# A curvature-flow stage on Trainium2: the step is clipped and the image rounded on GpSimd, the update comes one slot later, and the mixed derivative last

## Chip, cores and metric

One core of a Trainium2 chip. The metric is the device time of one execution in microseconds (us); lower is better. Everything is float32; the stencil matmuls read rounded copies in the format fp32r.

## Reference

Four blocks follow one another on a batch of 16 images of 16 channels and 32 x 32 pixels: an attention block with large weights (some 160 MB are read), two residual convolution blocks, and the curvature flow that the change is mostly about:

```python
def step(u, _):
    ux, uy, uxx, uxy, uyy = _derivs(u)          # Sobel stencils, each clipped to +-10
    g2 = ux * ux + uy * uy
    denK = jnp.maximum(1.0 + g2, EPS)
    K = jnp.clip((uxx * uyy - uxy * uxy) / (denK * denK + EPS), -5.0, 5.0)
    denH = jnp.sqrt(1.0 + g2 + EPS)
    H = ((1.0 + uy*uy) * uxx - 2.0 * ux*uy*uxy + (1.0 + ux*ux) * uyy) / (2.0 * denH**3 + EPS)
    H = jnp.clip(H, -5.0, 5.0)
    diff = jnp.clip(alpha * K + beta * H, -1.0, 1.0)
    u = u + DT * diff
    u = jnp.pad(u[:, :, 1:-1, 1:-1], ((0, 0), (0, 0), (1, 1), (1, 1)), mode='edge')
    return (u, None)
u, _ = jax.lax.scan(step, x, None, length=10)
return 0.7 * u + 0.3 * x
```

## The kernel before

**Weights and convolutions.** SyncE streams the weights through a ring of four 4 MB slots. TensorE consumes them (`thin`, L373); the last 16 blocks `s_` are the output projection. Between them the four convolution layers run in four waves of image columns (`conv`, matmuls at L497 and L502, relu L954 on ScalarE, add L776 on VectorE). `halo_rows` copies border rows between partition groups (L81, L85, L942), and `convs_after(s_)` says which layer follows which block. The last wave can only begin when the last block has arrived.

**Into the curvature stage.** `chunk_rows` (L509) gathers the images into four chunks `x` of 128 partitions (4 channels x 32 rows) by 32 columns x 16 images, the first half of the columns ahead of the last wave and the second behind it; L948, L864 and L1023 copy them out of PSUM into `u`. An image is held as a rounded high part (`u_hi`) and the rest (`u_lo`, L1076, GpSimd), so that two fp32r matmuls give nearly full precision. The stencil matrices are loaded by SyncE and cast to fp32r on GpSimd (L1070).

**The slots.** 10 steps x 4 chunks are 40 slots `k`. A slot of TensorE (`fields`, L548) is 34 matmuls of 480 columns: UXY 8, UX 4 and UY 6 (signal `fld1`), then UYY and UXX 16 (`fld2`), in that order. Each of the other engines runs its own `slot_step(k)` in which the front of slot k ("new") and the end of slot k-1 ("old") are interleaved in a written order; semaphores of the same names tie the engines together. The names are used in what follows:
- VectorE: `num0` L804 (old), `clip1` L807, `clipxy` L809, `clip2` L813, `kh` L820 (old), `slope` L825, `outer` L829, `cross` L835, then `diff` L841, `clipd` L844 and the update `u` L850 (old). clip1, clip2, kh and outer have 960 columns, the others 480.
- ScalarE: `p2` L986, `sqr` L987, `pad` L968 and the rounding `hi` L979 of the chunk for slot k+2, `up_h` L995, `end_k` L996, `ends` L1000 (old), `sqxy` L1005, `lnw` L1007, `psq` L1008, `w15` L1010, `lnd` L1013, `inv` L1016, and in the first four slots `x3` L1019 (0.3 u for the result).
- GpSimd: `absum` L1086 and `hn` L1088 (old, behind the update u of the slot before), `cxy` L1091, `m` L1093, `lo` L1076.

`num0` waits for `sqxy` and `m` of the slot before, `kh` for `hn` and `inv`, `diff` for `ends`, TensorE's next-but-one slot for `kh`. Two sets of buffers and of PSUM banks alternate (`q`, `n`).

**The tail.** TensorE applies the edge rule (L590), VectorE adds 0.3 x (L878, "finish"), SyncE stores.

## Time and profile before

| | us |
|---|---|
| median of 3 runs | 792.9 |
| lowest, highest | 789.88, 798.36 |
| the profiled execution, its own time | 793.43 |
| its span, first to last instruction | 791.6 |
| busy: TensorE, VectorE, ScalarE, GpSimd | 661.2, 463.0, 391.0, 269.1 |

The span is what the profile shows; the time has 1.8 us around it. The busy times are over the whole span, in which the first half is bound by weight transfers (DMA 32% of the chain that ended last); the curvature stage fills roughly the second half. In the views below a time is counted from the span's start.

### The profile page before, as it was taken

Reading aid. Unit: us, or ns where it says so; the run is one execution under the profiler, and the core shown is the slowest. Engines: PE = TensorE matmul, PEld = TensorE weight load, DVE = VectorE, ACT = ScalarE, POOL = GpSimd, SP = SyncE. Lnnn points to the kernel's source line nnn. Section 1 sums busy time; section 2 is a strip of 40 time slices with the busy share of each in tenths; the row PEclk is TensorE's granted clock in tenths of the full one; section 3 lists DMA queues with packets and bytes.
Section 4 is the critical chain, followed back from the end, with each engine's and each line's share of the span. In section 5 each row is a group of like instructions: output and inputs, shape, how many; then the busy total and the mean of one; then the engine's idle time right before and its main releaser. Section 6 shows DMA issues by size and latency. Waiting matters only on the chain.

```text
span 791.6 us, 11654 instructions
## 1 busy us (share of the span) xinstructions
PE 661.2 (84%) x4644; PEld 488.1 (62%) x4644; DVE 463.0 (58%) x668; ACT 391.0 (49%) x654; POOL 269.1 (34%) x231
## 2 busy tenths in 40 slices
PE   5896999998955588878789988989989988998983
PEld 3773874663522255555577777777767777777770
DVE  5630000491301022223253899999999999999996
ACT  1300000330000010111122899999999999999994
POOL 1000000000026000000011666776776677677662
PEclk9999999999986899999999999999999999999996
...
DMA packets 20804, 166.57 MB, mean 210 GB/s; under 512 B 1824, under 2 KB 1952, under 8 KB 11424
## 3 DMA queue, kind: packets, MB, share of 16 engines
...
## 4 chain that ended last, share of the span: by engine, by line
DMA 32%; PE 30%; ACT 16%; DVE 16%; issue 5%; POOL 1%; DVEq 0%; POOLq 0%; ACTq 0%; SPq 0%
DMA ring<-wout_w 19%; PE bank L548 10%; PE bank L359 6%; PE bank L419 4%; PE bank L474 3%; DMA ring<-wv_w 3%; PE bank L373 3%; DMA ring<-wv_p 3%; DMA ring<-wout_p 3%; DMA ring<-wqk_p 3%; DVE ring L820 3%; ACT ring L1000 3%; DVE ring L807 2%; ACT ring L996 2%; ACT bank L987 2%
## 5 line engine op out<-in xcount | busy, mean ns | idle before, releaser
L548 PE MATMUL bank<-u_parts,vmr 128*128 128x480 f32 x1360 | 305.3, 382 | 38.6 <-DVE ring L820 37.6
L548 PEld LDWEIGHTS bank<-u_parts,vmr 128*128 128x128 f32 x1360 | 252.7, 188 | 91.3 <-DVE ring L820 52.9
L373 PE MATMUL bank<-ring,small 128*32 128x256 f32 x1152 | 79.7, 426 | 36.0 <-DMA ring<-wout_w 32.1
L1086 POOL TENSOR_TENSOR ring<-ring 128x480 f32<-128x480 f32 x40 | 49.1, 1228 | 99.5 <-DVE reg_a L850 77.1
L373 PEld LDWEIGHTS bank<-ring,small 128*32 128x32 f32 x1152 | 37.9, 120 | 72.0 <-DMA ring<-wout_w 32.0
L373 PE MATMUL bank<-ring,xw 128*32 128x256 f32 x1024 | 62.3, 402 | 17.1 <-DMA ring<-wv_w 17.1
L784 DVE STREAM_TRANSPOSE reg_b<-bank 128x256 f32<-128x256 f32 x16 | 7.2, 450 | 109.7 <-PE bank L373 109.7
L942 ACT ACTIVATE reg_e<-xa 32x384 f32<-32x384 f32 (+9 forms) x16 | 8.3, 522 | 112.7 <-DVE xa L787 83.8
L671 DVE SCALAR_TENSOR_TENSOR reg_a<-bank,prm 128x512 f32<-128x512 f32 x4 | 2.8, 692 | 102.9 <-PE bank L426 102.9
L359 PE MATMUL bank<-reg_a,ring 128*128 128x256 f32 x256 | 57.9, 389 | 5.7 <-ACT reg_a L896 3.4
L373 PEld LDWEIGHTS bank<-ring,xw 128*32 128x32 f32 x1024 | 33.7, 115 | 43.8 <-DMA ring<-wv_w 20.8
L359 PEld LDWEIGHTS bank<-reg_a,ring 128*128 128x128 f32 x256 | 49.6, 195 | 13.3 <-issue 3.5
L1070 POOL CAST vmr<-ring 128x3328 fp32r<-128x3328 f32 x1 | 3.0, 2957 | 151.5 <-DMA ring<-edge 151.5
L1042 POOL MEMSET reg_d<- 128x2176 f32 x1 | 1.9, 1923 | 149.0 <-PE bank L426 149.0
L1088 POOL TENSOR_TENSOR ring<-ring 128x480 f32<-128x480 f32 x40 | 49.0, 1225 | 3.1
L1091 POOL TENSOR_TENSOR ring<-ring 128x480 f32<-128x480 f32 x40 | 48.8, 1219 | 3.4 <-DVE ring L807 3.4
L1093 POOL TENSOR_TENSOR ring<-ring 128x480 f32<-128x480 f32 x40 | 48.7, 1218 | 3.3 <-DVE ring L813 3.3
L807 DVE TENSOR_SCALAR ring<-bank 128x960 f32<-128x960 f32 x40 | 46.1, 1151 | 5.0 <-PE bank L548 5.0
L813 DVE TENSOR_SCALAR ring<-bank 128x960 f32<-128x960 f32 x40 | 46.0, 1149 | 2.7 <-PE bank L548 2.7
L820 DVE TENSOR_TENSOR ring<-ring,bank 128x960 f32<-128x960 f32 x40 | 45.8, 1146 | 0.9 <-POOL ring L1088 0.9
L829 DVE SCALAR_TENSOR_TENSOR ring<-bank,ring 128x960 f32<-128x960 f32 x40 | 46.0, 1149 | 0.0
L1076 POOL TENSOR_TENSOR u_parts<-reg_a,u_parts 128x512 fp32r<-128x512 f32 (+1 forms) x30 | 39.6, 1320 | 18.0 <-ACT u_parts L974 18.0
(186 smaller groups left out, 1020.7 us busy)
## 6 DMA issues: line engine op xcount, KB each, us to landing
...
```

Source lines behind the costliest of these rows:

```text
L359: ins = te.matmul(bank[:, 4 + n % 2, (h % 2) * TOK:(h % 2 + 1) * TOK], half[2 * (k % NSLOT) + h // 4][:, c, h % 4 * DH:(h % 4 + 1) * DH], ...
L373: ins = te.matmul(bank[32 * j:32 * j + 32, b_, n0:n0 + 256], lhs(c), slot[k % NSLOT][:, c, 256 * j:256 * j + 256], start=start and c == 0, ...
L548: last = te.matmul(dst[:, 0:NF], mat(m, first), p3[:, 2 + off:S + off, :], start=(high and n == 0), stop=(not high and n == len(terms) - 1))
L807: v.tensor_scalar(f(q, 0, 2).rearrange("p (x n) -> p x n", x=2), fields_in(q, 0, 2), 10.0, -10.0, ALU.min, ALU.max).then_inc(ve["clip1"], 1)
L813: v.tensor_scalar(f(q, 3, 2).rearrange("p (x n) -> p x n", x=2), bank[:, 3:5, 0:NF], 10.0, -10.0, ALU.min, ALU.max).then_inc(ve["clip2"], 1)
L820: v.tensor_tensor(kh[n].rearrange("p (x n) -> p x n", x=2), num[n].rearrange("p (x n) -> p x n", x=2), fields_in(n, 0, 2), ALU.mult).then_ ...
L829: v.scalar_tensor_tensor(ab[q].rearrange("p (x n) -> p x n", x=2), fields_in(q, 0, 2), 1.0, f(q, 3, 2).rearrange("p (x n) -> p x n", x=2), ...
L1076: p.tensor_tensor(u_lo[c][:, at], u[c][:, at], u_hi[c][:, at].bitcast(F32), ALU.subtract).then_inc(po["lo"], 1)
L1086: p.tensor_tensor(abs_[n], ab[n][:, 0:NF], ab[n][:, NF:2 * NF], ALU.add).then_inc(po["absum"], 1)
L1088: p.tensor_tensor(num[n][:, NF:2 * NF], abs_[n], cxy[n], ALU.add).then_inc(po["hn"], 1)
L1091: p.tensor_tensor(cxy[q], fld[q][:, 0:NF], fld[q][:, NF:2 * NF], ALU.mult).then_inc(po["cxy"], 1)
L1093: p.tensor_tensor(mxy[q], fld[q][:, 3 * NF:4 * NF], fld[q][:, 4 * NF:5 * NF], ALU.mult).then_inc(po["m"], 1)
```

## The change

It reorders the slot and moves two pieces of work to GpSimd.
- `clipd` becomes one GpSimd `tensor_scalar` (subtract `mid`, min DT); the other limit goes into the update, which is now max(dif, -DT) + u. `dif` gets two buffers.
- The update u of slot k-2 is made in slot k, between clip1 and clip2, instead of in slot k-1 at the end. GpSimd waits for it behind the clip.
- The rounding `hi` is a GpSimd copy ahead of `lo`, instead of a ScalarE step.
- `ends` is written to PSUM, into the bank of the mixed term (`mixed`), and `diff` reads it there. `diff` stands ahead of `cross`, which is now the slot's last step.
- TensorE makes UXY last in a slot (signal `fldxy`); clipxy is behind kh. On ScalarE, sqxy is behind w15.
- The stencil matrices go by a DMA of GpSimd's queue straight to `vmr`; the cast is gone.
- Convolution layer 1 follows layer 0 within one block, the first halves of the chunks are gathered one block earlier, the second halves chunk by chunk, and high and low parts are made by halves (FIRST, SECOND).
- The edge rule and the finish work on 30 columns and two rim columns; the last chunk goes in two parts.

The diff, cut to its core (8 leading blanks taken off):

```diff
@@ -64,7 +64,7 @@
     if s == NO - 1:
 return [(WAVES - 1, layer) for layer in range(NCONV)]
-    return [(w, s - G + 1 - G * w) for w in range(WAVES - 1) if 0 <= s - G + 1 - G * w < NCONV]
+    return [(w, layer) for w in range(WAVES - 1) for layer in range(NCONV) if s == G * (w + 1) - 1 + max(layer - 1, 0)]
 def halo_rows(eng, copy, shifts, w, layer, source, waits, halo_sem):
...
+def parts(x):
+    return [(2, S)] if x < NCH - 1 else [(2, S // 2 + 1), (S // 2 + 1, S)]
...
-vm = ring[:, la[0]:la[0] + NVM]
...
-end_k, up_h, end_h = dual(NF), dual(NF), dual(NF)
-dif = reg_b[:, 0:NF]
+end_k, up_h, dif = dual(NF), dual(NF), dual(NF)
 assert la[0] <= NSLOT * SLOTF
...
@@ -514,31 +526,33 @@
         i, m = s_ // NSLOT, s_ % NSLOT
         te.wait_ge(ve["bank_turn"], s_ + 1)
         thin(k1 + s_, lambda c: wft[:, c * 2 * B:(c + 1) * 2 * B], 4 + m, 0, True, True, s_ == NO - 1)
-        if s_ == NO - 1:
+        if s_ == NO - 2:
             te.wait_ge(po["pick"], 1)
             te.wait_ge(ve["conv"], pairs_done(WAVES - 2, NCONV - 1, 1))
             for x in range(NCH):
-                te.wait_ge(ve["bank_turn"], NO + x + 1)
+                te.wait_ge(ve["bank_turn"], NO + min(x, 2) + 1)
                 for g in range(G):
                     ins = chunk_rows(x, g, 0)
                 ins.then_inc(pe["chunk"], 1)
         for w, layer in convs_after(s_):
             if layer == 0:
                 te.wait_ge(ve["stage"], G * (w + 1))
+            if (w, layer) == (WAVES - 1, 0):
+                te.wait_ge(ac["u_in"], NCH)
...
     te.wait_ge(ac["u_in"], NCH)
-    for h in range(2):
-        te.wait_ge(ve["conv"], pairs_done(WAVES - 1, NCONV - 1, h))
-        for x in range(NCH):
-            for g in (2 * h, 2 * h + 1):
-                ins = chunk_rows(x, g, 1)
-            if h:
-                ins.then_inc(pe["chunk"], 1)
+    te.wait_ge(ve["bank_turn"], NO + NSLOT)
+    for x in range(NCH):
+        for g in range(G):
+            if x == 0 and g % 2 == 0:
+                te.wait_ge(ve["conv"], pairs_done(WAVES - 1, NCONV - 1, g // 2))
+            ins = chunk_rows(x, g, 1)
+        ins.then_inc(pe["chunk"], 1)
...
-        te.wait_ge(ac["hi"], k)
-        if reuse:
-            te.wait_ge(ve["num"], k - 2)
-        stencil(bank[:, b1 + 2, :], u_hi[c], first, UXY, True)
-        te.wait_ge(po["lo"], k)
-        stencil(bank[:, b1 + 2, :], u_lo[c], first, UXY, False)
+        if first:
+            te.wait_ge(ac["hi"], k)
+        else:
+            te.wait_ge(po["hi"], k - NCH)
         if reuse:
             te.wait_ge(ve["kh"], k - 2)
-        for n, terms in enumerate((UX, UY)):
-            stencil(bank[:, b1 + n, :], u_hi[c], first, terms, True)
-            ins = stencil(bank[:, b1 + n, :], u_lo[c], first, terms, False)
-        ins.then_inc(pe["fld1"], 1)
+        stencil(bank[:, b1, :], u_hi[c], first, UX, True)
+        te.wait_ge(po["lo"], k)
+        stencil(bank[:, b1, :], u_lo[c], first, UX, False)
+        stencil(bank[:, b1 + 1, :], u_hi[c], first, UY, True)
+        stencil(bank[:, b1 + 1, :], u_lo[c], first, UY, False).then_inc(pe["fld1"], 1)
...
-    te.wait_ge(po["vm"], 1)
-    te.wait_ge(ld_vm, 32)
+        if reuse:
+            te.wait_ge(ve["diff"], k - 2)
+        stencil(bank[:, b1 + 2, :], u_hi[c], first, UXY, True)
+        stencil(bank[:, b1 + 2, :], u_lo[c], first, UXY, False).then_inc(pe["fldxy"], 1)
+    te.wait_ge(ld_vm, 16)
...
-        te.wait_ge(ac["pad"], SLOTS - NCH + x + 1)
-        te.matmul(bank[:, EDGE_BANK[x], :], edge_m, u_in(x), start=True, stop=True).then_inc(pe["edge"], 1)
+        te.wait_ge(ve["u"], SLOTS - NCH + x + 1)
+        for n, (a_, b_) in enumerate(parts(x)):
+            te.matmul(bank[:, EDGE_BANK[x] + n, 0:(b_ - a_) * B], edge_m, u[x][:, a_ * B:b_ * B],
+                      start=True, stop=True).then_inc(pe["edge"], 1)
...
         n = 1 - q
+        mixed = lambda s_: fields_in(s_, 2)[:, 0, :]
         if old:
             v.wait_ge(po["m"], k - 1)
             v.wait_ge(ac["sqxy"], k - 1)
-            v.tensor_tensor(num[n][:, 0:NF], mxy[n], fields_in(n, 2)[:, 0, :], ALU.subtract).then_inc(ve["num"], 1)
+            v.tensor_tensor(num[n][:, 0:NF], mxy[n], mixed(n), ALU.subtract).then_inc(ve["num"], 1)
...
-            v.tensor_scalar(fields_in(q, 2)[:, 0, :], fields_in(q, 2)[:, 0, :], 10.0, -10.0,
-                            ALU.min, ALU.max).then_inc(ve["clipxy"], 1)
+        if before:
+            v.wait_ge(po["clipd"], k - 2)
+            if first and k - 2 <= NCH:
+                v.wait_ge(ac["x3"], k - 2)
+            inner = u[c][:, 2 * B:S * B]
+            v.scalar_tensor_tensor(inner, dif[q], -DT, inner, ALU.max, ALU.add).then_inc(ve["u"], 1)
...
+            v.wait_ge(pe["fldxy"], k)
+            v.tensor_scalar(mixed(q), mixed(q), 10.0, -10.0, ALU.min, ALU.max).then_inc(ve["clipxy"], 1)
...
+        if old:
+            v.wait_ge(ac["ends"], k - 1)
+            v.scalar_tensor_tensor(dif[n], end_k[n], ten_ab[:, 0:1], mixed(n),
+                                   ALU.min, ALU.add).then_inc(ve["diff"], 1)
+        if new:
             v.wait_ge(po["cxy"], k)
             v.wait_ge(ve["clipxy"], k)
-            v.scalar_tensor_tensor(cxy[q], cxy[q], -2.0, fields_in(q, 2)[:, 0, :],
-                                   ALU.mult, ALU.mult).then_inc(ve["cross"], 1)
-        if not old:
-            return
-        v.wait_ge(ac["ends"], k - 1)
-        v.scalar_tensor_tensor(dif, end_k[n], ten_ab[:, 0:1], end_h[n],
-                               ALU.min, ALU.add).then_inc(ve["diff"], 1)
-        v.wait_ge(ve["diff"], k - 1)
-        v.tensor_scalar(dif, dif, high_lim, low_lim, ALU.min, ALU.max).then_inc(ve["clipd"], 1)
-        v.wait_ge(ve["clipd"], k - 1)
-        if first and k - 1 <= NCH:
-            v.wait_ge(ac["x3"], k - 1)
-        inner = u[c][:, 2 * B:S * B]
-        v.scalar_tensor_tensor(inner, dif, mid, inner, ALU.subtract, ALU.add).then_inc(ve["u"], 1)
+            v.scalar_tensor_tensor(cxy[q], cxy[q], -2.0, mixed(q), ALU.mult, ALU.mult).then_inc(ve["cross"], 1)
...
+    def finish(x):
+        v.wait_ge(ac["x3"], x + 1)
+        x3c = x3[:, x, :].rearrange("p (w b) -> p w b", b=B)
+        for n, (a_, b_) in enumerate(parts(x)):
+            v.wait_ge(pe["edge"], x + n + 1)
+            got = bank[:, EDGE_BANK[x] + n, 0:(b_ - a_) * B].rearrange("p (w b) -> p w b", b=B)
+            inner = x3c[:, a_ - 1:b_ - 1, :]
+            v.scalar_tensor_tensor(inner, got, 0.7, inner, ALU.mult, ALU.add).then_inc(ve["fin"], 1)
...
+                  halo_waits(w, layer), ac["halo"])
+        if (w, layer) == (WAVES - 1, NCONV - 1):
+            a.wait_ge(pe["slot_used"], U_ALL)
+            a.wait_ge(ac["u_in"], NCH)
+            for x in range(NCH):
+                a.activation(u_hi[x][:, FIRST], u[x][:, FIRST], ACT.Copy).then_inc(ac["hi_first"], 1)
...
-            a.activation(u_hi[c], u[c], ACT.Copy).then_inc(ac["hi"], 1)
+            a.activation(u_hi[c][:, SECOND], u[c][:, SECOND], ACT.Copy).then_inc(ac["hi"], 1)
...
         pad(k - NCH, c)
-        a.wait_ge(ac["pad"], k - NCH)
-        a.wait_ge(pe["fld2"], k - NCH)
-        a.activation(u_hi[c][:, B:(S + 1) * B], u_in(c), ACT.Copy).then_inc(ac["hi"], 1)
...
-            a.activation(end_h[n], up_h[n], ACT.Relu, bias=ten_ab[:, 1:2],
+            a.activation(fields_in(n, 2)[:, 0, :], up_h[n], ACT.Relu, bias=ten_ab[:, 1:2],
                          scale=neg_b).then_inc(ac["ends"], 1)
...
-        a.wait_ge(ve["cross"], k)
-        a.activation(fields_in(q, 2)[:, 0, :], fields_in(q, 2)[:, 0, :], ACT.Square).then_inc(ac["sqxy"], 1)
         a.wait_ge(ve["slope"], k)
         a.activation(lnw[q], slope[q], ACT.Ln, bias=D_EPS).then_inc(ac["lnw"], 1)
         a.activation(den[q][:, 0:NF], slope[q], ACT.Square).then_inc(ac["psq"], 1)
         a.wait_ge(ac["lnw"], k)
         a.activation(den[q][:, NF:2 * NF], lnw[q], ACT.Exp, bias=LN2, scale=1.5).then_inc(ac["w15"], 1)
+        a.wait_ge(ve["cross"], k)
+        a.activation(fields_in(q, 2)[:, 0, :], fields_in(q, 2)[:, 0, :], ACT.Square).then_inc(ac["sqxy"], 1)
...
-    p.wait_ge(ld_vm, 32)
-    p.tensor_copy(vmr[:, :], vm).then_inc(po["vm"], 1)
+    p.wait_ge(pe["slot_used"], U_ALL)
+    p.dma_start(vmr[:, :], vmats).then_inc(ld_vm, 16)
+    p.wait_ge(ac["hi_first"], NCH)
+    p.wait_ge(ac["halo"], 2 * WAVES * NCONV)
+    p.wait_ge(ve["halo"], 4 * WAVES * NCONV)
+    for x in range(NCH):
+        p.tensor_tensor(u_lo[x][:, FIRST], u[x][:, FIRST], u_hi[x][:, FIRST].bitcast(F32),
+                        ALU.subtract).then_inc(po["lo_first"], 1)
...
-        p.wait_ge(ac["hi"], k)
-        at = slice(B, (S + 1) * B) if later else slice(0, ROWF)
+        at = slice(B, (S + 1) * B) if later else SECOND
+        if later:
+            p.wait_ge(ac["pad"], k - NCH)
+            p.wait_ge(pe["fldxy"], k - NCH)
+            p.tensor_copy(u_hi[c][:, at], u[c][:, at]).then_inc(po["hi"], 1)
+            p.wait_ge(po["hi"], k - NCH)
+        else:
+            p.wait_ge(ac["hi"], k)
         p.tensor_tensor(u_lo[c][:, at], u[c][:, at], u_hi[c][:, at].bitcast(F32),
                         ALU.subtract).then_inc(po["lo"], 1)
...
         if old:
-            if after:
-                p.wait_ge(ve["u"], k - 2)
-            p.wait_ge(ve["cross"], k - 1)
+            p.wait_ge(ve["outer"], k - 1)
             p.tensor_tensor(abs_[n], ab[n][:, 0:NF], ab[n][:, NF:2 * NF], ALU.add).then_inc(po["absum"], 1)
             p.wait_ge(po["absum"], k - 1)
+            p.wait_ge(ve["cross"], k - 1)
             p.tensor_tensor(num[n][:, NF:2 * NF], abs_[n], cxy[n], ALU.add).then_inc(po["hn"], 1)
+        if before:
+            p.wait_ge(ve["diff"], k - 2)
+            if k == 3:
+                p.wait_ge(ve["scales"], 1)
+            p.tensor_scalar(dif[q], dif[q], mid, DT, ALU.subtract, ALU.min).then_inc(po["clipd"], 1)
+            p.wait_ge(ve["u"], k - 2)
```

## Rows read from the trace of the kernel before

**Rows 1.** Windows view, a stretch of the curvature stage; engine, busy us, instructions.

```profile
600.00:650.00 50.00, 44.25 (x198) 36.51 (x197) 49.31 (x65) 48.10 (x77) 34.91 (x29) 1.00 0.00 0
```

**Rows 2.** Timeline, vector engine: start, length, engine, line, operation, tiles.

```profile
600.52 1.15 DVE L820 TENSOR_TENSOR ring<-ring,bank 128x960 f32<-128x960 f32 x1
...
609.12 1.15 DVE L820 TENSOR_TENSOR ring<-ring,bank 128x960 f32<-128x960 f32 x1
```

**Rows 3.** Timeline of one early slot, all engines; brackets give idle time and releaser.

```profile
444.44 1.14 DVE L820 TENSOR_TENSOR ring<-ring,bank 128x960 f32<-128x960 f32 x1
...
445.96 0.59 ACT L995 ACTIVATE ring<-ring 128x480 f32<-128x480 f32 x1
...
446.46 0.77 ACT L996 ACTIVATE ring<-ring,small 128x480 f32<-128x480 f32 x1
...
447.32 0.79 ACT L1000 ACTIVATE ring<-ring,small 128x480 f32<-128x480 f32 x1
448.02 0.55 ACT L1005 ACTIVATE bank<-bank 128x480 f32<-128x480 f32 x1
...
448.51 0.58 ACT L1007 ACTIVATE ring<-ring 128x480 f32<-128x480 f32 x1
...
449.46 0.72 DVE L850 SCALAR_TENSOR_TENSOR reg_a<-reg_b,small,reg_a 128x480 f32<-128x480 f32 x1
449.49 0.59 ACT L1010 ACTIVATE ring<-ring 128x480 f32<-128x480 f32 x1
450.10 0.65 DVE L804 TENSOR_TENSOR ring<-ring,bank 128x480 f32<-128x480 f32 x1
...
450.26 1.23 POOL L1086 TENSOR_TENSOR ring<-ring 128x480 f32<-128x480 f32 x1 [2.77 <-DVE reg_a L850]
450.67 1.15 DVE L807 TENSOR_SCALAR ring<-bank 128x960 f32<-128x960 f32 x1
...
451.58 1.23 POOL L1088 TENSOR_TENSOR ring<-ring 128x480 f32<-128x480 f32 x1
451.73 0.66 DVE L809 TENSOR_SCALAR bank<-bank 128x480 f32<-128x480 f32 x1
...
453.36 1.15 DVE L820 TENSOR_TENSOR ring<-ring,bank 128x960 f32<-128x960 f32 x1
...
455.11 1.30 POOL L1076 TENSOR_TENSOR u_parts<-reg_a,u_parts 128x512 fp32r<-128x512 f32 x1
```

**Rows 4.** Timeline of the first slot: the mixed term's square and its reader.

```profile
439.35 0.56 ACT L1005 ACTIVATE bank<-bank 128x480 f32<-128x480 f32 x1 [3.46 <-DVE ring L835]
...
440.01 0.66 DVE L804 TENSOR_TENSOR ring<-ring,bank 128x480 f32<-128x480 f32 x1 [0.69 <-ACT bank L1005]
```

**Rows 5.** GpSimd's groups by line: busy us, mean ns, idle before.

```profile
L1070 POOL CAST vmr<-ring 128x3328 fp32r<-128x3328 f32 x1 | 3.0, 2957 | 151.5 <-DMA ring<-edge 151.5
...
L1064 POOL COPY prm<-prm 128x128 f32<-128x128 f32 x1 | 0.3, 302 | 0.0
```

**Rows 6.** Timeline from the last weights to the first stencils.

```profile
399.37 1.91 PE L509 MATMUL bank<-xa,prm 128*32 128x256 f32 x32
...
407.00 3.62 DVE L85 COPY reg_f<-reg_d 16x480 f32<-16x480 f32 x2
...
410.77 1.63 PE L502 MATMUL bank<-reg_f,xw 96*128 96x160 f32 x8 [1.74 <-DVE reg_f L85]
...
414.12 1.06 DVE L85 COPY reg_e<-xa 16x528 f32<-16x528 f32 x2
...
429.17 15.87 PE L548 MATMUL bank<-u_parts,vmr 128*128 128x480 f32 x72 [0.22 <-POOL u_parts L1076]
```

**Rows 7.** Timeline of the tail.

```profile
780.58 1.16 DVE L820 TENSOR_TENSOR ring<-ring,bank 128x960 f32<-128x960 f32 x1 [0.89 <-POOL ring L1088]
781.77 0.60 ACT L995 ACTIVATE ring<-ring 128x480 f32<-128x480 f32 x1 [1.52 <-DVE ring L820]
...
788.49 0.69 DVE L878 SCALAR_TENSOR_TENSOR ring<-bank,ring 128x512 f32<-128x512 f32 x1 [1.89 <-PE bank L590]
```

More of the change, by code:

```diff
@@ L85, in halo_rows, with chunk_bank @@
         copy(halo[dw * QUAD:dw * QUAD + C, 0:G - 1, at], cols(slice(0, C), 1, G, dw)).then_inc(halo_sem, 1)
+def parts(x):
+    return [(2, S)] if x < NCH - 1 else [(2, S // 2 + 1), (S // 2 + 1, S)]
+def chunk_bank(x, half):
+    return 4 + x if half or x < NCH - 1 else 0
 def pairs_done(w, layer, h):
@@ L186, in build @@
         dt_ab, five_ab, ten_ab = (sm(2) for _ in range(3))
-        neg_b, mid, low_lim, high_lim = (sm(1) for _ in range(4))
+        neg_b, mid = (sm(1) for _ in range(2))
         wft = sm(KC * 2 * B)
@@ L201, in build @@
             "pl_sq_sums", "pln", "negmax", "prob", "pf", "dsl", "stage", "conv", "bank_turn", "img",
-            "clip1", "clipxy", "clip2", "num", "slope", "outer", "cross", "kh", "diff", "clipd", "u", "scales", "fin", "halo", "u_in")}
+            "clip1", "clipxy", "clip2", "num", "slope", "outer", "cross", "kh", "diff", "u", "scales", "fin", "halo", "u_in")}
         ac = {n: sem("ac_" + n) for n in (
             "order", "patch_sq", "patch_std", "fl", "win_sq", "win_std", "pl_std", "qkv", "vt", "exp", "pt", "rows",
-            "wwk", "wv", "conv", "p2", "sqr", "sqxy", "lnw", "psq", "w15", "lnd", "inv", "end_k", "up_h", "ends", "x3", "pad", "hi", "halo", "u_in")}
-        po = {n: sem("po_" + n) for n in ("zero", "bandz", "pick", "vm", "padz", "lo", "cxy", "m", "absum", "hn")}
+            "wwk", "wv", "conv", "p2", "sqr", "sqxy", "lnw", "psq", "w15", "lnd", "inv", "end_k", "up_h", "ends", "x3", "pad", "hi", "hi_first", "halo", "u_in")}
+        po = {n: sem("po_" + n) for n in ("hi", "clipd", "zero", "bandz", "pick", "padz", "lo", "lo_first", "cxy", "m", "absum", "hn")}
         ld_last, st_out = [sem(f"ld_last{n}") for n in range(NPIECE)], sem("st_out")
@@ L582, in _ @@
                     fields(i * NCH + (c + 1), c, False, True)
+            te.wait_ge(ld_edge, 16)
             for x in range(NCH):
@@ L857, in _ @@
             then(v.tensor_scalar(neg_b, dt_ab[:, 1:2], -1.0, None, ALU.mult))
-            then(v.tensor_tensor(mid, five_ab[:, 0:1], five_ab[:, 1:2], ALU.add))
-            then(v.tensor_scalar(low_lim, mid, DT, None, ALU.subtract))
-            v.tensor_scalar(high_lim, mid, DT, None, ALU.add).then_inc(ve["scales"], 1)
+            v.tensor_tensor(mid, five_ab[:, 0:1], five_ab[:, 1:2], ALU.add).then_inc(ve["scales"], 1)
             for x in range(1, NCH, 2):
@@ L1098, in _ @@
                 low(x + 1, x, False)
-            for k in range(1, LOOP_FROM):
-                slot_step(k, k % 2, (k + 1) % NCH, True, k > 1, k > 2, k + 2 > NCH)
-            with p.Fori(1, LOOPS + 1) as i:
-                for m in range(NCH):
-                    slot_step(i * NCH + (m + 3), (m + 3) % 2, (m + 4) % NCH, True, True, True)
-            for k in range(LOOP_END, SLOTS + 2):
-                slot_step(k, k % 2, None, k <= SLOTS, True, True)
+            for k in range(1, SLOTS + 3):
+                slot_step(k, k % 2, (k + 1) % NCH if k + 2 <= SLOTS else None, k <= SLOTS, 1 < k <= SLOTS + 1, k > 2, k + 2 > NCH)
     return nc
```

53 lines of the change are left out of this document (28 added, 25 removed).

## Prediction, made before the changed kernel was run

> **What bounds the kernel now.** I read the busy times of a stretch in the middle of the curvature stage first: of 50 us the vector engine is busy 49.3, ScalarE 48.1, TensorE 44.3 and GpSimd 34.9 [rows 1]. Two engines are nearly full, so the view of busy times can't say what a lighter load on one of them is worth; that depends on who waits for whom. Next the timeline: the same instruction of the vector engine, the product `kh` (L820), starts every 8.60 us [rows 2]. The stage is 40 such slots, and what counts is the period. The last view is one slot read start to start, since instructions of one engine overlap by a tenth of a microsecond and their printed lengths add up to too much [rows 3]. Start to start, a vector step of 960 columns takes 1.06 (450.67 to 451.73), one of 480 takes 0.57 (450.10 to 450.67), and `u`, with two operands in SBUF, 0.64 (449.46 to 450.10) [rows 3]. Before the stage, the chip waits for the output weights and then for the last wave of convolutions; behind it there is one serial tail.
>
> **The vector engine's own work.** The change takes `clipd` (L844) from it and the second SBUF operand from `diff`. What is left is clip1, clip2, kh and outer at 1.06, num0, clipxy, slope, diff and cross at 0.57, and u at 0.64: 4.24 + 2.85 + 0.64 = 7.73 us, 0.87 under the period of now. If nothing else became late, 38 slots of that would be worth 33 us. ScalarE loses the rounding `hi` (L979, some 0.6 with its launch), so it has room too.
>
> **The wait that takes the place.** `num0` of slot k+1 needs the square of the mixed term, `sqxy(k)`, from ScalarE, which needs `cross(k)`. Before, cross was followed on the vector engine by diff, clipd and u, which hid the square. After, cross is the last step of slot k and num0 the first of the next, with nothing between. And on ScalarE, sqxy is no longer ahead of lnw but behind `up_h`, `end_k`, `ends`, `lnw`, `psq` and `w15`, all in order. The first of these waits for kh. That closes a ring, and I count round it, from the start of kh(k-1), start to start where an engine follows itself:
> kh to the start of up_h: 1.15 long [rows 3] and 0.03 to get across, as in the last slot, where ScalarE waited for it (780.58 + 1.16 to 781.77 [rows 7]), so 1.18; up_h to end_k 0.50, end_k to ends 0.86 (it drains first), ends to the next instruction 0.70 [rows 3]. With PSUM as target I take 0.65: `sqxy` in PSUM takes 0.55 to 0.56 against 0.58 to 0.60 for the like work into SBUF [rows 3, 4]. lnw and psq together 0.98 (448.51 to 449.49), w15 0.49, the half of that [rows 3]. sqxy to the start of num0: 0.66 [rows 4], the only place before where the vector engine waited for it. Then num0 0.57, clip1 1.06, u 0.64, clip2 1.06 [rows 3], and kh(k) may start.
> Sum: 1.18 + 0.50 + 0.86 + 0.65 + 0.98 + 0.49 + 0.66 + 0.57 + 1.06 + 0.64 + 1.06 = 8.65. The only term without a row is ends into PSUM, 0.60 to 0.70, which makes 8.60 to 8.70. So the vector engine gets 7.7 us of work in a slot and stands idle 0.9 us, ahead of num0. I expect 8.65 where 8.60 was.
>
> **GpSimd.** It takes two instructions more. The rounding copy of 512 columns has a price from two rows: a copy of 128 columns takes 0.302 and the cast of 3,328 takes 2.957 [rows 5], 0.83 ns a column, so 0.62. The clip (`tensor_scalar`, 480 columns, one scalar from memory) has no row. Its lower end is the same line, 0.59. Its upper end is the two-operand step, 1.23 [rows 3], with 0.09 for the scalar from memory (end_k, with two such scalars, takes 0.77 where up_h takes 0.59 [rows 3]), so 1.32. It streams one tensor, as the copies do, and so I take 0.59 + 0.09 = 0.68.
> The Trainium skill (GPSIMD Engine Reference, Engine selection) speaks against moving elementwise work here: two-input work is about twice as slow as on VectorE, while one-input work goes at roughly line rate. By its first half the clip would be the 1.23 of the rows, by its second half near the copies' line; the trace has the two-operand steps at 1.23 and no clip, so it bears out the first and leaves the second open for this operation. The first would make the time 799.6, the second leaves it at 788.6.
> Two rings go through GpSimd. One: u start to cxy 0.80 (449.46 to 450.26, since GpSimd waits for u), cxy and m 1.18 each (451.58 to 455.11 is three steps at 1.18), hi 0.62 + 0.08, lo 1.27 (its 1.30 less the overlap), absum 1.32, hn 1.18, then the clip X and 0.08 to u: 7.71 + X [rows 3]. Two: outer 1.15 + 0.08, absum 1.32, hn 1.18, X + 0.08, u 0.64, clip2 1.06, kh 1.06, clipxy and slope 1.14: 7.71 + X again. With X = 0.68 both give 8.39, hidden under 8.65; they decide from X = 0.94 on, and their cover is 0.26 us. Behind the clip in GpSimd's queue are cxy, m, hi and lo, and for these wait cross, num0 and TensorE two slots on; the fields of slot k+2 have more than 5 us of slack, since u one slot later still comes 2 slots ahead of its use.
>
> **TensorE.** It issues the same 34 matmuls a slot in another order. 72 of them ran without a break in 15.87 us [rows 6], 0.22 each, so 7.5 us a slot, below every ring. UXY last means it waits for diff(k-2) and clip2(k-1), but is needed only by clipxy, a step after kh. I price that at nothing; the cover is about 3.9 us of lead.
>
> **Start of the stage.** Three gains. (a) The first half of the images is gathered one weight block earlier, while DMA is the bound. Of the 32 passes with 1.91 us at 399.37 [rows 6] about 0.8 stood past the point where the convolution could begin (estimate; ends 0.4 to 1.9). (b) The cast of the stencil matrices, 2.96 us on GpSimd, goes away. It became possible when the matrices had landed, just then two small halo copies of the vector engine (407.00) took 3.62 us, and a like pair later 1.06; TensorE was idle for 1.74 on them [rows 5, 6]. That the two engines were in each other's way is my reading. Gain 1.7, or nothing if it was something else. The matrices come by a DMA from GpSimd's queue to their final place instead; the 22 us from 407.00 to 429.17 hide it. (c) Chunks in order of x, and a second-half-only rounding: the first low part is ready about 1.1 sooner, and 64 matmuls between it and the second clip2 become 58 (estimate from the order: 6 x 0.22 = 1.3). Together 0.8 + 1.7 + 2.4 = 4.9, so kh(1), at 444.44 [rows 3], comes at 439.5.
>
> **The slots.** kh(39) is 38 periods on: 439.5 + 38 x 8.65 = 768.2. The four slots in which ScalarE also stores 0.3 u ran at 8.92 before (444.44 to 453.36 [rows 3]) and don't now, since ScalarE has about 7.7 of own work. That is 1.0 us of the gain. kh(40) comes without clip1 and clip2 in the way: about 7.3 on, 775.5, against 780.58 [rows 7].
>
> **The tail.** Before, from kh(40) to the end of the last vector step 788.49 + 0.69 - 780.58 = 8.60 [rows 7]. After: ends' result at 3.3, diff to 4.0, finish(0) and finish(1) in the vector queue to 5.5 (the clip on GpSimd ends at 4.8 and is hidden), u to 6.2, two edge matmuls of 240 columns at about 1.0 each, then finish: 8.9. So 0.3 is lost; smaller last transfers may give it back. Last vector step at 784.4, plus the 2.4 of the output DMA before (span 791.6 less 789.18): span 786.8. The profiled execution took 793.43 for 791.6 of span, so 1.8 more: 788.6. That stands against 793.43 of the profiled execution and against the median of 792.9.
>
> **The rivals.**
> Forecast (chance 0.60): the ring over sqxy, 8.60 to 8.70 a slot, 788.6; with the start's bounds 785 to 792.
> GpSimd becomes the bound (0.14). Mechanism: the clip costs as a two-operand step and u waits for it. Point of decision X = 0.94. With 1.23 the period is 8.94 and the time 788.6 + 38 x 0.29 = 799.6; with 1.32 it is 9.03 and 803. This is slower than before. For it speaks that no GpSimd arithmetic at less than 1.22 is on record in this trace, against it the copies.
> The mixed square isn't late (0.14). If sqxy ran beside the rest, or ScalarE's steps were closer together than in the slow first slots, GpSimd at 8.39 would be next: 788.6 - 38 x 0.26 = 778.7. Half of that, 784, is as possible. Against it speaks the code: the order on both engines is fixed.
> The start gives nothing (0.12). Mechanism: GpSimd's descriptor work for the matrices and its four early low parts run beside the same vector copies as the cast did, so gains (b) and part of (c) don't come: 791 to 794.
> The Trainium skill (SBUF — State Buffer, Who interferes with whom) has GpSimd and a two-port VectorE operation exclude each other; by its rule the descriptors, not the vector copies, could be the ones to wait, and the time would stay at the forecast.
>
> **How the numbers follow.** About 1% (8 us) is what a measurement of this kernel can tell from no change. The faster side (under 785) takes most of the third rival and a little of the forecast: 0.22. The slower side (over 801) takes the upper half of the second and a little for what I missed: 0.13. The range 779 to 802 holds the forecast, the fourth, and all but the ends of the others.
>
> **What would show it.** In the profile after: the vector engine idle about 0.9 us ahead of num0 in each slot, released by ScalarE's square; vector engine busy near 90%, ScalarE near 90%, GpSimd above 85%; kh every 8.65; the chain of waits alternating between ScalarE's six steps and num0, clip1, u, clip2, kh. kh(1) near 439.5, halo copies at 1.1 a pair. I am wrong if u waits for GpSimd's clip (X over 0.94), if hi takes over 0.9, or if kh comes sooner than every 8.6.

## The result, and the profile after

| | before | after |
|---|---|---|
| median, us | 794.07 (4 runs, 789.88 to 798.36) | 833.08 (4 runs, 830.67 to 835.23) |
| the profiled execution, us | 793.43 | 833.83 |
| its span, us | 791.6 | 832.0 |

The kernel after takes 1.050 times as long as the one before [1.046, 1.0535, the 95% interval]. The forecast was 788.6, the range 779 to 802.

The page of the kernel after: busy times, and three groups of the list by line (busy us and mean ns of one, then the engine's idle time ahead of them and what ended it).

```profile
PE 690.2 (83%) x4646; PEld 511.7 (61%) x4646; DVE 441.6 (53%) x632; ACT 362.0 (44%) x618; POOL 364.8 (44%) x311
...
L562 PE MATMUL bank<-u_parts,vmr 128*128 128x480 f32 x1360 | 323.3, 398 | 58.0 <-DVE ring L848 57.3
...
L1133 POOL TENSOR_SCALAR ring<-ring,small 128x480 f32<-128x480 f32 x40 | 75.5, 1888 | 4.8 <-DVE ring L865 4.8
...
L1125 POOL TENSOR_TENSOR ring<-ring 128x480 f32<-128x480 f32 x40 | 49.0, 1226 | 7.9 <-DVE ring L859 6.1
```

L1133 is the clip on GpSimd: 1.89 us, the only GpSimd step above 1.3 in the slot, and more than the two-input sum of the same 480 columns (L1125, 1.23). One slot of the timeline, the steps around it (start us, length us, engine, line; in brackets the idle time before and its releaser); it answers to [rows 2, 3]:

```profile
619.24 1.14 DVE L848 TENSOR_TENSOR ring<-ring,bank 128x960 f32<-128x960 f32 x1
...
620.44 7.62 PE L562 MATMUL bank<-u_parts,vmr 128*128 128x480 f32 x34 [0.58 <-DVE ring L848]
620.55 0.61 POOL L1113 CAST u_parts<-reg_a 128x512 fp32r<-128x512 f32 x1
...
621.80 0.76 ACT L1030 ACTIVATE bank<-ring,small 128x480 f32<-128x480 f32 x1
622.49 0.59 ACT L1035 ACTIVATE ring<-ring 128x480 f32<-128x480 f32 x1
...
624.01 1.24 POOL L1128 TENSOR_TENSOR ring<-ring 128x480 f32<-128x480 f32 x1
...
624.62 0.65 DVE L827 TENSOR_TENSOR ring<-ring,bank 128x480 f32<-128x480 f32 x1 [0.76 <-ACT bank L1040]
...
625.22 1.89 POOL L1133 TENSOR_SCALAR ring<-ring,small 128x480 f32<-128x480 f32 x1
...
627.14 0.66 DVE L838 SCALAR_TENSOR_TENSOR reg_a<-ring,reg_a 128x480 f32<-128x480 f32 x1 [0.80 <-POOL ring L1133]
...
627.89 1.20 POOL L1138 TENSOR_TENSOR ring<-ring 128x480 f32<-128x480 f32 x1 [0.78 <-DVE reg_a L838]
...
628.79 1.15 DVE L848 TENSOR_TENSOR ring<-ring,bank 128x960 f32<-128x960 f32 x1
```

From `kh` (L848) to `kh` are 9.55 us where 8.60 were. Inside the slot both waits are to be seen: `num0` (L827) waits 0.76 for the square, forecast as about 0.9, and `u` (L838) waits 0.80 for the clip, which the forecast had hidden and the prediction had named as the sign that it is wrong; GpSimd then waits 0.78 for `u`. That the second sets the period is what experiments 1 and 2 show. From 600 to 650 us VectorE is busy 42.0 us, ScalarE 38.2 and GpSimd 44.6: 84%, 76% and 89%, where near 90%, near 90% and above 85% were forecast. The view of waits, whole span (total us, times, longest):

```profile
PE bank L562 <- DVE ring L848: 57.3, 38, 2.3
...
DVE ring L827 <- ACT bank L1040: 30.3, 40, 0.8
...
DVE reg_a L838 <- POOL ring L1133: 25.0, 30, 1.8
```

The other 10 of the 40 updates go to `reg_g` and wait 7.9 us more.

**The balance.** kh(1) comes at 445.28 (before 444.44 [rows 3]), kh(39) at 812.02, kh(40) at 820.46 (before 780.58 [rows 7]); the span ends 11.54 later (before 11.02). So 0.84 + 39.04 + 0.52 = 40.4 us, all that lies between 793.43 and 833.83, nearly all of it in the slots. Of the 38 intervals from kh(1) to kh(39), 25 take 9.53 to 9.55 and 13 take 9.83 to 9.88. The view by stretches shows what is with 12 of the 13 (the other, the 15th, has a clock of 1.00 and comes up in experiment 6); here a usual interval and the long one after it (busy us of each engine, PEclk, DMA share, GB/s):

```profile
464.40:473.90 9.50, 7.63 (x34) 6.30 (x34) 7.94 (x11) 7.98 (x13) 8.50 (x8) 1.00 0.00 0
473.90:483.80 9.90, 8.60 (x32) 7.35 (x33) 8.09 (x12) 7.45 (x12) 8.85 (x8) 0.83 0.00 0
```

In the 12 the granted clock is 0.83 in the mean (for part of the interval 1.2 GHz, the lower level), after TensorE had waited 2.0 us for kh (L848) at 475.20; the fields come late and clip2 (L841) waits for them at its end:

```profile
475.20 8.99 PE L562 MATMUL bank<-u_parts,vmr 128*128 128x480 f32 x33 [2.01 <-DVE ring L848]
...
482.71 1.16 DVE L841 TENSOR_SCALAR ring<-bank 128x960 f32<-128x960 f32 x1 [0.25 <-PE bank L562]
```

**The start.** The halo copies that took 3.62 [rows 6] take 1.00, and the matmuls behind them no longer wait: the cast had been in their way. But the first convolution of the last wave takes 5.50 us where the same 24 matmuls took 3.21, at a clock of 0.50 (1.2 GHz):

```profile
402.78 1.94 PE L385 MATMUL bank<-ring,small 128*32 128x256 f32 x16 [0.53 <-DMA ring<-wout_w]
...
405.61 5.50 PE L509 MATMUL bank<-xa,reg_c 128*128 128x144 f32 x24 [0.90 <-DVE xa L809]
...
413.70 1.00 DVE L85 COPY reg_f<-reg_d 16x480 f32<-16x480 f32 x2
```

```profile
400.00:410.00 10.00, 8.26 (x50) 5.58 (x51) 2.55 (x6) 1.12 (x2) 0.57 (x1) 0.50 0.46 164
```

### The profile page after: what moved, and what is told of

It reads as the page before. It is cut to its first block, busy times and chain, and to the rows that moved or that the text cites. A ratio compares the mean times of both kernels' runs of the same rounds, so it can differ in the third digit from the quotient of the medians.

```text
span 832.0 us, 11664 instructions
## 1 busy us (share of the span) xinstructions
PE 690.2 (83%) x4646; PEld 511.7 (61%) x4646; DVE 441.6 (53%) x632; ACT 362.0 (44%) x618; POOL 364.8 (44%) x311
## 4 chain that ended last, share of the span: by engine, by line
PE 36%; DMA 27%; POOL 20%; DVE 12%; issue 4%; ACT 1%; SPq 0%; POOLq 0%; DVEq 0%; ACTq 0%
DMA ring<-wout_w 18%; PE bank L562 12%; PE bank L371 7%; POOL ring L1133 6%; PE bank L385 5%; POOL ring L1128 4%; POOL ring L1125 4%; DVE ring L848 4%; PE bank L486 4%; PE bank L431 3%; DMA ring<-wv_w 3%; DMA ring<-wout_p 3%; DMA ring<-wqk_p 3%; PE bank L509 2%; DVE ring L841 2%
## 5 line engine op out<-in xcount | busy, mean ns | idle before, releaser
L562 PE MATMUL bank<-u_parts,vmr 128*128 128x480 f32 x1360 | 323.3, 398 | 58.0 <-DVE ring L848 57.3
L562 PEld LDWEIGHTS bank<-u_parts,vmr 128*128 128x128 f32 x1360 | 267.0, 199 | 114.4 <-issue 59.2
L1133 POOL TENSOR_SCALAR ring<-ring,small 128x480 f32<-128x480 f32 x40 | 75.5, 1888 | 4.8 <-DVE ring L865 4.8
L371 PE MATMUL bank<-reg_a,ring 128*128 128x256 f32 x256 | 61.9, 407 | 5.9 <-ACT reg_a L925 3.4
L371 PEld LDWEIGHTS bank<-reg_a,ring 128*128 128x128 f32 x256 | 52.4, 206 | 14.9 <-issue 3.5
L1025 ACT ACTIVATE ring<-ring 128x480 f32<-128x480 f32 x40 | 24.2, 605 | 77.5 <-DVE ring L848 77.5
L1125 POOL TENSOR_TENSOR ring<-ring 128x480 f32<-128x480 f32 x40 | 49.0, 1226 | 7.9 <-DVE ring L859 6.1
L841 DVE TENSOR_SCALAR ring<-bank 128x960 f32<-128x960 f32 x40 | 46.1, 1153 | 5.5 <-PE bank L562 5.5
```

What stands on the lines that cost most here:

```text
L371: ins = te.matmul(bank[:, 4 + n % 2, (h % 2) * TOK:(h % 2 + 1) * TOK], half[2 * (k % NSLOT) + h // 4][:, c, h % 4 * DH:(h % 4 + 1) * DH], ...
L562: last = te.matmul(dst[:, 0:NF], mat(m, first), p3[:, 2 + off:S + off, :], start=(high and n == 0), stop=(not high and n == len(terms) - 1))
L841: v.tensor_scalar(f(q, 3, 2).rearrange("p (x n) -> p x n", x=2), bank[:, 3:5, 0:NF], 10.0, -10.0, ALU.min, ALU.max).then_inc(ve["clip2"], 1)
L1125: p.tensor_tensor(abs_[n], ab[n][:, 0:NF], ab[n][:, NF:2 * NF], ALU.add).then_inc(po["absum"], 1)
L1133: p.tensor_scalar(dif[q], dif[q], mid, DT, ALU.subtract, ALU.min).then_inc(po["clipd"], 1)
```

## The experiments

Each was run beside the kernel before (its median 794.75, 795.34 and 793.32 us in the three groups). In later kernels the line numbers are a few higher or lower.

**1. The clip back on VectorE (v_clip).** All else is as changed.

```diff
-  # GpSimd, slot k:
-    p.wait_ge(ve["diff"], k - 2)
-    p.tensor_scalar(dif[q], dif[q], mid, DT, ALU.subtract, ALU.min).then_inc(po["clipd"], 1)
+  # VectorE, last in slot k, behind cross:
+    v.wait_ge(ve["diff"], k - 1)
+    v.tensor_scalar(dif[n], dif[n], mid, DT, ALU.subtract, ALU.min).then_inc(ve["clipd"], 1)
```

> The changed kernel with one thing undone: the clip (subtract, min) is a VectorE instruction again, last in the slot behind cross, and leaves GpSimd. Theory A (GpSimd's clip of 1.89 us is the whole loss; behind it stands the ring over the square sqxy): the clip falls into the 0.76 us that VectorE waits ahead of num0, the period goes from 9.54 to 8.65, GpSimd's own ring is about 7.7; the time is 445.3 (first kh) + 38 x 8.65 + 7.3 + 10.4 (tail) + 1.8 = 793. Theory B (the later update and the rounding copy load GpSimd too much, whatever the clip): the period stays above 9.2 and the time above 815. Theory C (VectorE and GpSimd are in each other's way once an SBUF-to-SBUF clip of VectorE runs beside absum and hn): the clip stretches by up to 1.2 us, the period is 9.1 to 9.4, the time 810 to 822.

792.76 us, ratio 0.997 [0.995, 1.000]. Every interval is 8.65 to 8.67: the ring over the square, counted as 8.65. The clip takes 0.47 on VectorE and lies in the wait for the square, of which 0.38 is left:

```profile
614.30 0.47 DVE L874 TENSOR_SCALAR ring<-ring,small 128x480 f32<-128x480 f32 x1
...
615.15 0.66 DVE L827 TENSOR_TENSOR ring<-ring,bank 128x480 f32<-128x480 f32 x1 [0.38 <-ACT bank L1043]
```

So the clip on GpSimd makes all of the loss; the rest of the change is worth about nothing. Theory A had 793; of theory C there is no sign, since every clip of this run took 0.46 or 0.47.

**2. The square early (sq_early).** The clip stays on GpSimd; cross goes ahead of diff, and the square ahead of lnw.

```diff
   # VectorE
+  cross; then diff              (was: diff; then cross)
   # ScalarE
+  a.activation(mixed, mixed, ACT.Square).then_inc(ac["sqxy"], 1)
   a.activation(lnw[q], slope[q], ACT.Ln, bias=D_EPS).then_inc(ac["lnw"], 1)
   ...
-  a.activation(mixed, mixed, ACT.Square).then_inc(ac["sqxy"], 1)   # was behind w15
```

> The changed kernel with the order of the mixed term's square undone and the clip left on GpSimd: cross ahead of diff on VectorE, sqxy ahead of lnw on ScalarE. Theory A (GpSimd's ring decides, sqxy's wait of 0.76 us lies under it): the wait ahead of num0 goes away, the wait ahead of u grows by as much (from 0.80 to 1.5), the period stays at 9.54 and the time at 831 to 834. Rival (the wait for sqxy is what costs): the period falls by 0.6 to 0.76, the time is 804 to 810.

827.76 us, ratio 1.0425 [1.038, 1.047]; period 9.50. `num0` no longer waits, and the time goes to the other wait: `u` waits 1.54 for the clip. The time is some 3 us under the 831 to 834 of theory A: in the profiles kh(1) comes 3.0 us sooner than as changed (442.28) and the 38 intervals take 2.0 less.

```profile
640.15 1.89 POOL L1133 TENSOR_SCALAR ring<-ring,small 128x480 f32<-128x480 f32 x1
...
642.07 0.66 DVE L838 SCALAR_TENSOR_TENSOR reg_a<-ring,reg_a 128x480 f32<-128x480 f32 x1 [1.54 <-POOL ring L1133]
```

**3. What the price of the clip is made of (g_imm, g_one, g_half).**

```diff
-  p.tensor_scalar(dif[q], dif[q], mid, DT, ALU.subtract, ALU.min)
+  p.tensor_scalar(dif[q], dif[q], 0.0055, DT, ALU.subtract, ALU.min)                          # g_imm
+  p.tensor_scalar(dif[q], dif[q], mid, None, ALU.subtract)                                    # g_one
+  p.tensor_scalar(dif[q][:, 0:NF // 2], dif[q][:, 0:NF // 2], mid, DT, ALU.subtract, ALU.min) # g_half
```

> The changed kernel with an immediate (0.0055) in the clip where the scalar mid is read from memory; mid enters the result in this form only for the default parameters. What the scalar costs. Theory 1 (the second arithmetic step is dear): the instruction stays at 1.8 us or more, the time at 830 to 834. Theory 2 (the scalar from memory is dear): it falls to 0.6 to 1.2 us, the period by as much down to 8.65 to 8.9, the time 795 to 808.

> The changed kernel with only the subtraction in GpSimd's instruction, the scalar still from memory; the upper limit of the step (DT) is left out of the computation. Theory 1 (the second step is dear): the instruction falls to 0.6 to 1.2 us, the time to 795 to 808. Theory 2 (the scalar from memory is dear): it stays at 1.8 us, the time at 830 to 834.

> The changed kernel, with GpSimd clipping only the first 240 of the 480 columns; the other half of the step is left unclipped, so that part of the computation is left out. If the clip's 1.89 us is a price per column, it takes about 1.0 us, the two GpSimd rings fall from 9.54 to about 8.65 to 8.7 us, where the ring over the square takes over, and one run takes 793 to 797 us. If most of it is a fixed price of this instruction, it stays at 1.6 to 1.9 us and the time at 820 to 833.

`g_one` and `g_half` leave part of the clip out. One run of each, and the clip's group in each (in this order):

```profile
L1133 POOL TENSOR_SCALAR ring<-ring 128x480 f32<-128x480 f32 x40 | 72.7, 1818 | 4.8 <-DVE ring L865 4.8
```

```profile
L1133 POOL TENSOR_SCALAR ring<-ring,small 128x480 f32<-128x480 f32 x40 | 59.4, 1485 | 4.8 <-DVE ring L865 4.8
```

```profile
L1133 POOL TENSOR_SCALAR ring<-ring,small 128x240 f32<-128x240 f32 x40 | 43.5, 1089 | 4.8 <-DVE ring L865 4.8
```

| | clip, us | usual period | period less clip | time, us |
|---|---|---|---|---|
| half the columns | 1.089 | 8.74 | 7.65 | 794.7 |
| one step | 1.485 | 9.13 | 7.65 | 811.42 |
| immediate | 1.818 | 9.46 | 7.64 | 827.12 |
| as changed | 1.888 | 9.54 | 7.65 | 833.08 |

Four prices give one line: period = clip + 7.65, where the prediction had 7.71 + X. The scalar from memory costs 0.07 and the second step 0.40. `g_one` fits neither theory: 1.485 lies between 0.6 to 1.2 and 1.8, and 811.42 between the two times. `g_imm` keeps its price as in theory 1; its time is under 830 since kh(1) came 2.7 us sooner (442.57) and the 38 intervals take 3.8 less. From 240 to 480 columns the price rises by 0.80, 3.3 ns a column; if the price is a straight line between these two widths, 0.29 are fixed. The price per column is four times that of GpSimd's copies (0.83 [rows 5]).

**4. Both undone (both), and GpSimd without the wait for u (both_nowait).** `both` is 1 and 2 together; `both_nowait` also takes `p.wait_ge(ve["u"], k - 2)` away from GpSimd, whose next steps there use nothing of u's.

> Both undone together: the clip back on VectorE (last in the slot) and the square early (cross ahead of diff, sqxy ahead of lnw). Theory (two rings lie one under the other, GpSimd's at 9.54 and the square's at 8.66): the square alone gave nothing, the clip alone left 8.66, and together VectorE's own work is next, 7.73 + 0.56 = 8.3 a slot; time 792.8 - 38 x 0.36 = 779, 2% under the kernel before. Rival (something else stands at 8.66, such as TensorE's wait for kh): the period stays at 8.6 to 8.66 and the time at 790 to 793.

> As both, and GpSimd no longer waits for the update u ahead of cxy, so that its two-operand steps run beside u, which has two operands in SBUF. If the two engines shut each other out, u (0.65) or the GpSimd step beside it stretches by up to 1.2 us, and as VectorE is the bound the period rises from 8.3 towards 8.5 or more, time 785 to 800. If they share, the period stays within 0.03 of that of both.

`both` 783.48 us, ratio 0.985 [0.981, 0.990]; `both_nowait` 781.39, 0.985 [0.980, 0.990]. Behind the first four intervals the period is 8.28 to 8.33, 8.30 in the mean, in both. Now VectorE works without a gap: in the stretch from 600 to 650 us it is busy 49.8 of 50, where it was 42.0 as changed. `both` was expected at 779: the period came as expected, but three of the first intervals take 1.8 us more (9.59, 8.63, 8.45), and kh(40) follows kh(39) by 8.28, where it was 7.39 in `v_clip`. In the longest, the one behind kh(1), the clip started 0.02 us behind a GpSimd step and took 1.47 instead of 0.47.

```profile
450.54 1.22 POOL L1131 TENSOR_TENSOR ring<-ring 128x480 f32<-128x480 f32 x1
450.56 1.47 DVE L874 TENSOR_SCALAR ring<-ring,small 128x480 f32<-128x480 f32 x1
```

In the later slots of the same run the clip comes first, and takes 0.47 while the GpSimd step takes 1.40:

```profile
626.24 0.47 DVE L874 TENSOR_SCALAR ring<-ring,small 128x480 f32<-128x480 f32 x1
626.40 1.40 POOL L1131 TENSOR_TENSOR ring<-ring 128x480 f32<-128x480 f32 x1
```

Whoever starts first keeps its pace and the other is held up. The Trainium skill says that of the two engines (SBUF — State Buffer, Who interferes with whom): a `tensor_scalar` of VectorE in its two-port mode and GpSimd shut each other out for the whole instruction. The rows agree, 1.47 against 0.47. Without the wait for u GpSimd's first product runs beside `u`, which reads two SBUF tensors, and takes 1.58 instead of 1.22. The same section of the Trainium skill has a VectorE instruction with two SBUF inputs contend with a GpSimd instruction that reads SBUF, and the 1.58 agrees. That step isn't on the ring, so the period stays.

**5. The rounded copy back on ScalarE (both_hi).** As `both`, with

```diff
   # ScalarE, behind the pad of slot k - 4
+  a.activation(u_hi[c][:, B:(S + 1) * B], u_in(c), ACT.Copy).then_inc(ac["hi"], 1)
   # GpSimd
-  p.tensor_copy(u_hi[c][:, at], u[c][:, at]).then_inc(po["hi"], 1)
```

> The clip on VectorE last in its slot and the square early, with the rounded copy back on ScalarE: what moving the rounded copy alone is worth. Theory A: ScalarE's own work of one slot rises by the copy's 0.55 to 0.6 us to about 8.2, at or just under the period of 8.30, and the copy stands in the ring of the square: period 8.4 to 8.6, 787 to 795 us. Theory B: ScalarE still has room for it, and GpSimd's work falls: period 8.30 or less, 780 to 784 us, and moving the copy was worth nothing.

806.4 us, ratio 1.018 [1.016, 1.020]: 23 us above `both`, and neither theory had that. From the sixth on the intervals alternate, 8.28 and 9.41 (one of 9.87 is long by the clock). Here a long one and the short one after it, each from `kh` (L845) on; L867 is `diff`, L871 the clip, L1127 GpSimd's `hn`:

```profile
614.10 1.15 DVE L845 TENSOR_TENSOR ring<-ring,bank 128x960 f32<-128x960 f32 x1
...
618.22 0.71 DVE L867 SCALAR_TENSOR_TENSOR ring<-ring,small,bank 128x480 f32<-128x480 f32 x1 [0.21 <-ACT bank L1033]
...
618.83 1.23 POOL L1127 TENSOR_TENSOR ring<-ring 128x480 f32<-128x480 f32 x1
618.97 1.35 DVE L871 TENSOR_SCALAR ring<-ring,small 128x480 f32<-128x480 f32 x1
...
623.51 1.14 DVE L845 TENSOR_TENSOR ring<-ring,bank 128x960 f32<-128x960 f32 x1
...
627.33 0.70 DVE L867 SCALAR_TENSOR_TENSOR ring<-ring,small,bank 128x480 f32<-128x480 f32 x1
...
628.07 0.47 DVE L871 TENSOR_SCALAR ring<-ring,small 128x480 f32<-128x480 f32 x1
628.23 1.39 POOL L1127 TENSOR_TENSOR ring<-ring 128x480 f32<-128x480 f32 x1
```

GpSimd is not early: `hn` starts 4.73 behind kh in the long slot and 4.72 in the short one, and 4.73 in `both`. It is the clip that is late, 4.87 behind kh instead of 4.56 (4.57 in `both`), because `diff` waits 0.21 for `ends` (L1033) of ScalarE, which now has one step more to do in each slot. In `both` the clip leads `hn` by 0.16 only; 0.3 later it comes behind it, takes 1.35 instead of 0.47, and the slot takes 1.13 more. In that longer slot ScalarE catches up, and the next clip is in time again. 17 of the 40 clips took 1.34 to 1.46, and in 16 of these slots `diff` had waited for `ends` (the other is the one behind kh(1), long in `both` too). Three more intervals, with a clip of 0.47, are long by the clock, 0.83 in the mean. So theory A had the right engine, ScalarE, and missed what a small delay does there. All this is read from the rows; a run in which GpSimd waits for the clip, which would test it, was not made.

**6. The clock in the slots (slot_fill).** The changed kernel with four matmuls more in each slot:

```diff
                 if reuse:
+                    te.wait_ge(ve["clip2"], k - 1)
+                    for _ in range(4):
+                        te.matmul(bank[:, 3, 0:NF], mat("SV", first), <480 columns of u_hi[c]>, start=True, stop=True)
                     te.wait_ge(ve["kh"], k - 2)
```

> The changed kernel, with four more matmuls in each slot of the nodes: 480 columns each, into a bank that nobody reads, in the stretch in which TensorE waits about 2 us for the new tile of VectorE. Theory A: the 13 slots that took 9.83 to 9.88 instead of 9.54 us are those in which the granted clock fell to 0.5 while TensorE waited, and they vanish: every slot 9.54, 4.3 us less, about 829 us. Theory B: the long slots have another cause, and stay: 833 us. If the added matmuls get in the way of the step's own, the slot is longer than 9.54 in all rows.

825.89 us, ratio 1.042 [1.040, 1.044]. 12 of the 13 long intervals are gone, and the clock is 1.00 in all 38 (as changed 0.83 in these 12). kh(1) to kh(39) falls from 366.7 to 362.9. One interval of 9.84 stays, at a clock of 1.00; in it GpSimd's `hn` began 0.41 us after the step before it, where about 0.1 is usual:

```profile
579.82 1.23 POOL L1132 TENSOR_TENSOR ring<-ring 128x480 f32<-128x480 f32 x1 [0.41 <-POOL ring L1129]
```

It is the 15th interval in the changed kernel too, and the 15th is 0.3 above the usual one in `g_imm`, `g_one` and `g_half` as well (9.75, 9.44, 9.03). So it isn't the clock; what it is isn't settled. Another 4.1 us came at the start, where this run changes nothing: kh(1) at 441.19, see 7.

**7. The start (both_chunk, both_warm, best).** `both_chunk` gathers the first halves of the chunks behind the last weight block again (`s_ == NO - 1`); `both_warm` fills TensorE's waits in the last block with matmuls that nobody reads; `best` is `both_warm` without GpSimd's wait for u.

```diff
+  def fill(k, c, n):
+      for j in range(4 * n):
+          te.matmul(bank[32 * (j % 4):32 * (j % 4) + 32, 3, 0:256], <weights of piece c>, <256 columns>, start=True, stop=True)
...
   if pieces and c % (KC // NPIECE) == 0:
+      if c:
+          fill(k, c - 1, 2)
       te.wait_ge(ld_last[c // (KC // NPIECE)], 16)
```

> As both, with the first halves of the chunks gathered behind the last weight block again, where the kernel before had them. Theory (these 32 passes kept TensorE busy ahead of the last wave; without them it waits between the last pieces, the granted clock falls to 1.2 GHz and the first convolution takes 5.1 to 5.8 us where it took 3.2): the convolution takes 3.2 to 3.6 again, but begins 0.8 later; from the arrival of the last piece to the first kh it is 1 to 1.5 us shorter than in both. Rival (the clock falls there by chance): no difference in the convolution, 0.8 us longer in all. Either is at the edge of what the times can show; the profile decides.

> As both, with filler matmuls into an unused PSUM bank in the gaps of the last weight block (two groups of four per gap, three behind the last). They compute nothing that is used. Theory of the clock: the granted clock stays at its full level, the first convolution of the last wave takes 3.2 us, and the stage begins 2 us sooner than in both: 777. Rival: the fillers change nothing, or cost their own 0.5 us.

> The clip on VectorE last in its slot, the square early, filler matmuls in the gaps of the last block, and GpSimd not waiting for the update. By the two runs from which it is put together: start as with the filler matmuls alone, the first long interval after kh(1) gone or shorter, period 8.30, so 778 to 781 us, a ratio of about 0.98. The rival: the gain of either alone was the same microsecond or two of the start, and it stays at 781.

`both_chunk` 782.84 us, 0.9855 [0.981, 0.990]; `both_warm` 780.72, 0.9825 [0.9785, 0.9865]; `best` 781.11, 0.985 [0.983, 0.9875]. `both_warm` had been expected at 777, `best` at 778 to 781. The last weights arrive at another time in each execution, so I compare from the matmuls on the last piece to kh(1):

| | first convolution, us | last piece to kh(1), us |
|---|---|---|
| before | 3.21 | 45.96 |
| after | 5.50 | 42.50 |
| both | 5.81 | 43.28 |
| both_chunk | 3.18 | 43.01 |
| both_nowait | 4.85 | 41.45 |
| both_hi | 4.69 | 41.29 |
| v_clip, g_imm | 5.81, 5.80 | 42.81, 42.81 |
| sq_early | 5.08 | 42.58 |
| g_one | 3.21 | 39.83 |
| both_warm | 3.21 | 40.17 |
| best | 3.21 | 40.14 |
| slot_fill, g_half | 3.21 | 39.36, 39.33 |

The changed kernel's start takes 42.5 with the convolution at 5.50, and 39.3 with it at 3.21. To gather the chunks earlier takes work out of the last block, where TensorE then stands between the last pieces: by one profile of each it is worth 2.8 us with the clock up (`both_chunk` to `both_warm`) and next to nothing without (`both_chunk` to `both`, 0.3 us the other way, where 1 to 1.5 were expected). In `both` the clock from 400 to 410 is 0.51, in `both_warm` 1.00:

```profile
400.00:410.00 10.00, 8.25 (x52) 5.81 (x52) 2.54 (x6) 1.12 (x2) 0.57 (x1) 0.51 0.51 179
```

```profile
400.00:410.00 10.00, 9.90 (x99) 8.71 (x89) 4.48 (x10) 3.32 (x6) 0.57 (x1) 1.00 0.50 177
```

It isn't so in every execution: of ten profiles with the early gathering and no filler, seven had 4.69 to 5.81 and three had 3.21 (`slot_fill`, `g_half`, `g_one`). Both profiles with filler had 3.21, which two executions could also have by chance; so that the filler holds the clock up is likely and not shown. `best` brings nothing over `both_warm`, and the first long interval, 9.60, stayed. The profile of `both_nowait` has the period of `both`; what it is ahead lies at its start, 2.9 us by earlier weights and 1.8 between the last piece and kh(1).

## Why the prediction was wrong

**The step that failed** is the price X of the clip in the paragraph on GpSimd: "It streams one tensor, as the copies do, and so I take 0.59 + 0.09 = 0.68", with 1.32 as its upper end. It is 1.89. Both bounds came from other instructions, a copy and a two-input product, and the operation costs more than either; the rows had none of its kind. The rival "GpSimd becomes the bound" had the right mechanism and the right point of decision, and an end that was too low. Of the 1.21 us too little, 0.26 went into the cover, 0.06 into a ring counted too long, and 0.89 came through 38 times: 33.8 us of the 45.2 by which the forecast was off.

**The other terms.**
- The ring over the square, 8.65: measured 8.66 once the clip is off GpSimd (experiment 1). Its parts hold too: as changed `num0` waits 0.76 (30.3 us in 40 slots), and `ends` into PSUM to the next step is 0.69, in its bounds of 0.60 to 0.70.
- The rings through GpSimd, 7.71 + X: measured 7.65 + X for four prices. 0.06 too long, 2.3 us in 38 slots.
- The rounded copy, 0.62: 0.61. That taking it off ScalarE has an effect beyond its price, since it lets `ends` and `diff` come in time, the prediction didn't see (experiment 5).
- "The mixed square isn't late", 778.7: with the square early the next bound is VectorE at 8.30, not GpSimd at 8.39, and it takes both edits (experiment 4). VectorE's 7.73 holds: with 0.39 for the clip from start to start, and 0.74 instead of 0.57 from `diff` to the clip that reads it, it is 8.29.
- TensorE "at nothing": its order costs nothing (`both` has it too, and VectorE has no gap), but in the long slots, behind waits for kh of 1.9 to 2.3 us, its clock falls: 3.9 us in 12 intervals, which experiment 6 takes away. The 13th is 0.3 us with another cause.
- The start, 4.9: 6.6 where the clock stays up (45.96 to 39.3), 3.5 in the profiled execution (42.50). The halo copies at 1.00 without the cast bear out that it was in their way; part (a), taken as 0.8, is worth 2.8 by the two profiles of experiment 7. On top, the last weights came 4.3 us later than in the one profile of before; in the 13 profiles of the changed forms they came 1.0 to 4.3 later. Whether the change does that stays open. Together kh(1) is 5.8 later than forecast.
- kh(40) came 8.44 behind kh(39), not 7.3, and the tail is 11.54, not 11.3, since the clip isn't hidden there either: the last two `u` wait 1.83 and 0.76 for it. In `v_clip` kh(40) comes 7.39 behind kh(39).

The sum with these, the start, the clip, the 13 long intervals, kh(40) and the tail: 788.6 + 5.8 + 33.8 + 4.2 + 1.1 + 0.2 = 833.7 against 833.83.
